# Attention phase of a macaron block: another schedule of units, projections, sums and rotation on four engines

## The chip, the cores and the metric

The kernel runs on one core of one Trainium2 chip. The metric is the device time of one execution in microseconds. The engines are called as the profile calls them: PE (TensorE), DVE (VectorE), ACT (ScalarE), POOL (GpSimd) and SP (the queue that issues all DMAs here).

## The reference

The block computes, on x of 8 x 512 x 512 in fp32:

```python
x = x + 0.5 * ffn(layernorm(x))          # 2:4-sparsified SwiGLU, 512 -> 2048 -> 512
x = x + attention(layernorm(x))
x = x + 0.5 * ffn(layernorm(x))

# attention, 16 heads of 32, one shared key/value head
q = (x @ w_q.T) heads * 32**-0.5;  k, v = split(x @ w_kv.T);  k *= 32**-0.5
q, k = rotary_xpos(q, scale), rotary_xpos(k, 1 / scale)
out = softmax(where(causal, -max, q @ k.T)) @ v
out = out @ w_proj.T + b_proj
```

## The kernel before

Three phases follow one another: `ffn_phase`, `attention_phase`, `ffn_phase`. The change touches the second alone.

**Units.** The attention of one batch element (a "batch", B of 8) is 16 units. Four consecutive units are one group: four heads whose head dimensions fill the 128 partitions (`HG` = 4 heads, `NHG` = 4 groups a batch). Unit K of a group has one block of 128 query rows, row i = K % 4, against (i+1)·128 keys, so the four units of a group have 128, 256, 384 and 512 keys. K runs on through all batches (`ALL` = 128).

**One unit, engine by engine.** `scores(K)` (L871) is four fp32 matmuls, one per head, into banks 0 to 3 of PSUM; they wait until `mask_scores(K-1)` has emptied those banks. `mask_scores(K)` (L1143, DVE, operation at L1149) adds the causal mask, writes the scores to a slot of `probs` and their minimum to `nmax`. `exps(K, s)` (L1023, ACT, L1029) takes the exponential in place and sums the row. `turn_probs(K, j)` (L887, PE, L892) transposes each 128x128 block of the four heads into a turn bank. `copy_turned(K, j)` brings it to `pt`, on ACT (L1034) or, where `ON_VECTOR` says so, on DVE (L1155). `weigh(K)` (L895, matmuls L907) multiplies by the values into bank 6.

**The group's end.** `invert_sums` (DVE, L1161) takes the reciprocal of 16 sums, `widen` (ACT, L1040) spreads them to 128x512, `turn_sums` (PE, L868) transposes them, `drain_sums` (ACT, L1047) copies the result to `rt`, `scale_output` (DVE, L1168) multiplies bank 6 by `rt` into `att`. `cast_output` (ACT, L1051) and `low_output` (POOL, L764) split `att` into a high and a low part. The first `weigh` of the next group waits for `scale_output`.

**Side work.** While a batch is computed, PE also projects the next batch's keys/values (L826) and queries (L851, four row tiles) and the previous batch's output (L918, four row tiles): nine items of 12 matmuls 128x512. All go through one PSUM bank, `spare`. Each unit has four places (`side(K, 0..3)`); an item has a period of six places, with three matmuls in each of the first four. DVE empties `spare`: `rotate_q` (L1110 to L1112, three multiplications out of the bank, then an addition on POOL, L759) or `add_output` (L1173); ACT does it for the keys/values (L1005). The next item waits for that (`take_spare`). LayerNorm of the next batch (normalise, `turn_x`, high part on ACT at L242, low part on DVE at L237) sits in units 0 and 1 of each batch, four `turn_x` in all.

**Turn banks.** Banks 4 and 5 alternate for everything that PE transposes (`next_turn`, `take_turn`). A transpose waits until the bank's previous content has been drained, by whichever engine drains it.

**What sets the order.** Every engine has its own list of instructions, written out by hand in a function `step(K)`, and executes it strictly in that order. PE's step K is: side 0, [`turn_sums` of the previous group if i = 0], `turn_probs` 0 and 1, side 1, `weigh(K-1)`, `turn_probs` 2 and 3, side 2, `scores(K+2)`, side 3, then the turns of x, keys or queries. ACT's step K has the exponentials of K+1 with the copies of K between them; DVE's has the copies of K, then `mask_scores(K+2)`, and `scale_output` last if i = 0.

The lines that set the places:

```python
ON_VECTOR = ((), (1,), (1,), (1,))
TURN_X, TURN_KV, TURN_K, TURN_Q = (0, 1), 3, 6, (10, 11)
ROTATE = {5: 0, 6: 1, 8: 2, 9: 3}
SUM = {11: 0, 12: 1, 14: 2, 15: 3}
STATS = {7: (0,), 10: (1,), 13: (2, 3)}
```

Of the kernel before, what the change touches and what calls it, by code (L numbers as in the profile page):

```python
# [18 lines left out]
F32 = mybir.dt.float32  # L19
# [6 lines left out]
P = 128  # L26
# [4 lines left out]
def macaron_kernel(nc, x_in, w_gu, w_d, w_q, w_kv, w_p, b_p, rotary, out):  # L31
# [40 lines left out]
    nmax = place("nmax", [P, 2, TT], F32)  # L72
# [62 lines left out]
    with ExitStack() as ctx:  # L135
# [51 lines left out]
        q_done = sem("q_done")  # L187
        q_rotated = sem("q_rotated")
# [454 lines left out]
        def attention_phase(src, dst, m0):  # L643
# [27 lines left out]
            def blocks_before(K, of):  # L671

                one = [sum(1 for j in range(i + 1) if of(i, j)) for i in range(TT)]
                return K // TT * sum(one) + sum(one[:K % TT])
# [10 lines left out]
            def copies_of(K, j):  # L685

                mine = by_vector if by_vector(K % TT, j) else by_scalar
                return (pt_vector if mine is by_vector else pt_scalar,
                        blocks_before(K, mine) + sum(1 for n in range(j + 1) if mine(K % TT, n)))
# [10 lines left out]
            for hg in range(NHG):  # L700
                next_turn(("q", 0, hg))
            for K in range(ALL):
                nxt, k = K // UNITS + 1, K % UNITS
                if k % TT == 0 and K > 0:
                    next_turn(("r", K // TT - 1))
                for j in range(K % TT + 1):
                    next_turn(("p", K, j))
                if nxt < BATCHES:
                    if k in TURN_X:
                        next_turn(("x", nxt, 2 * k))  # L710
                        next_turn(("x", nxt, 2 * k + 1))
# [4 lines left out]
                    if k in TURN_Q:  # L716
                        next_turn(("q", nxt, 2 * (k - TURN_Q[0])))
                        next_turn(("q", nxt, 2 * (k - TURN_Q[0]) + 1))
            next_turn(("r", ALL // TT - 1))

            with nc.Block() as blk:
# [30 lines left out]
                def _(g):  # L752
# [4 lines left out]
                    def finish_q(B, t):  # L757
                        g.wait_ge(q_rotated, (B * TT + t + 1) * QSTEP)
                        g.tensor_tensor(qrot[:, t], qrot[:, t], qtmp[:, t % 2], ALU.add).then_inc(q_finished, 1)  # L759

                    def low_output(G):
                        h_of, l_of = att_of(G // NHG)
                        g.wait_ge(att_h_done, G + 1)
                        g.tensor_tensor(l_of[:, G % NHG], att[:, :], h_of[:, G % NHG].bitcast(F32), ALU.subtract).then_inc(att_l_done, 1)  # L764

                    def step(K):
                        B, k = divmod(K, UNITS)
                        nxt = B + 1
                        if k % TT == 1 and K > TT:
                            low_output(K // TT - 1)  # L770
                        if nxt < BATCHES:
                            if k == 3:
                                for t in range(TT):
                                    add_bias(nxt, t)
                            if k in ROTATE:
                                finish_q(nxt, ROTATE[k])
                        if k == 13 and B + 2 < BATCHES:
                            ln_gpsimd(g, B + 2 + m0, 0)
# [16 lines left out]
                def _(pe):  # L795
# [25 lines left out]
                    def project_kv(B, k):  # L821
                        if k == 0:
                            pe.wait_ge(xnt_done, (B + m0) * TT + TT)
                            take_spare(kvt_done, B + 1)
                        for n, (w, x) in enumerate(((wkv_h, xnt_h), (wkv_l, xnt_h), (wkv_h, xnt_l))):
                            last = pe.matmul(spare[0:2 * HD, :], w[:, k], x[:, 0, k], start=(k == n == 0),  # L826
                                             stop=(k == KD - 1 and n == 2))
                        if k == KD - 1:
# [17 lines left out]
                    def project_q(B, t, k):  # L846
                        if k == 0:
                            take_spare(q_rotated, (B * TT + t + 1) * QSTEP)
                        tok = slice(t * P, (t + 1) * P)
                        for n, (x, w) in enumerate(((xnt_h, wq_h), (xnt_h, wq_l), (xnt_l, wq_h))):  # L850
# [462 lines left out]
```

## Time and profile before

| | us |
|---|---|
| median of 3 runs | 2982.3 (2977.7 to 2983.5) |
| the profiled execution | 2983.71 |
| its span | 2981.9 |
| PE busy | 2794.2 (94%) |
| DVE busy | 1855.5 (62%) |
| ACT busy | 1200.8 (40%) |
| POOL busy | 157.0 (5%) |

The span runs from the first to the last instruction. Busy times overlap between engines. PE's clock is at one of two levels, 2.4 GHz (written 1.00) or 1.2 GHz (0.50); a row shows the mean of a stretch. The first FFN phase ends at about 1091 us, the attention ends at about 1891 us.

### The profile page before, as it was taken

Reading aid. Unit: us, or ns where it says so; the run is one execution under the profiler, and the core shown is the slowest. Engines: PE = TensorE matmul, PEld = TensorE weight load, DVE = VectorE, ACT = ScalarE, POOL = GpSimd, SP = SyncE. Lnnn points to the kernel's source line nnn. Section 1 sums busy time; section 2 is a strip of 40 time slices with the busy share of each in tenths; the row PEclk is TensorE's granted clock in tenths of the full one; section 3 lists DMA queues with packets and bytes.
Section 4 is the critical chain, followed back from the end, with each engine's and each line's share of the span. In section 5 each row is a group of like instructions: output and inputs, shape, how many; then the busy total and the mean of one; then the engine's idle time right before and its main releaser. Section 6 shows DMA issues by size and latency. Waiting matters only on the chain. (4 is left out here: it accounts for less than half of the span.)

```text
span 2981.9 us, 41915 instructions
## 1 busy us (share of the span) xinstructions
PE 2794.2 (94%) x15648; PEld 2213.2 (74%) x15648; DVE 1855.5 (62%) x3535; ACT 1200.8 (40%) x2527; POOL 157.0 (5%) x152
## 2 busy tenths in 40 slices
PE   7999999999999977788888887799999999999998
PEld 6888888888888855556555655588888888888887
DVE  5666666666756646555555555476766576676665
ACT  3323233333332315666666677233333333333232
POOL 0000000000000003111111110000000000000000
PEclk9999999999999988999999999899999999999999
DMA  3211211221121020000000000321131112112100
GB/s 131 82 43 57 85 43 46 79 96 49 53 75 43 14 108 1 1 29 11 20 30 29 15 8 16 120 75 49 46 127 43 42 58 85 50 46 90 56 14 29
DMA packets 65021, 156.11 MB, mean 52 GB/s; under 512 B 6864, under 2 KB 6992, under 8 KB 64592
## 3 DMA queue, kind: packets, MB, share of 16 engines
q1 hardware_dynamic: 64848, 153.77, 15.2%
q8 instruction: 112, 1.84, 0.3%
q14 instruction: 61, 0.50, 0.1%
HBM read 128.58 MB, written 25.17 MB: 52 GB/s over the span
## 5 line engine op out<-in xcount | busy, mean ns | idle before, releaser
L346 PE MATMUL bank<-xnt_h,wgu_h 128*128 128x512 f32 x2048 | 803.3, 392 | 10.3 <-issue 7.4
L346 PE MATMUL bank<-xnt_h,wgu_l 128*128 128x512 f32 x2048 | 798.9, 390 | 0.0
L346 PE MATMUL bank<-xnt_l,wgu_h 128*128 128x512 f32 x2048 | 798.4, 390 | 0.0
L503 DVE TENSOR_TENSOR h<-bank,sg 128x512 f32<-128x512 f32 x256 | 176.9, 691 | 600.4 <-PE bank L346 585.9
L346 PEld LDWEIGHTS bank<-xnt_h,wgu_h 128*128 128x128 f32 x2048 | 385.6, 188 | 91.5 <-issue 9.0
L442 ACT ACTIVATE mag<-h 128x512 f32<-128x512 f32 x256 | 162.0, 633 | 702.6 <-DVE h L503 702.6
L346 PEld LDWEIGHTS bank<-xnt_h,wgu_l 128*128 128x128 f32 x2048 | 385.3, 188 | 80.3
L346 PEld LDWEIGHTS bank<-xnt_l,wgu_h 128*128 128x128 f32 x2048 | 385.7, 188 | 79.2
L365 PE MATMUL bank<-wd_h,hs_h 128*128 128x512 f32 x1024 | 400.5, 391 | 9.1 <-DVE hs_l L538 9.1
L365 PE MATMUL bank<-wd_l,hs_h 128*128 128x512 f32 x1024 | 400.1, 391 | 0.0
L365 PE MATMUL bank<-wd_h,hs_l 128*128 128x512 f32 x1024 | 400.0, 391 | 0.0
L1149 DVE CUSTOM_DVE_ANT_0 probs<-bank,causal 128x384 f32<-128x384 f32 (+3 forms) x512 | 220.7, 487 | 230.2 <-PE bank L883 229.2
L450 ACT CAST hs_h<-h 128x512 fp32r<-128x512 f32 x256 | 155.5, 622 | 508.1 <-DVE h L532 508.1
L1029 ACT ACTIVATE probs<-probs,nmax 128x384 f32<-128x384 f32 (+3 forms) x512 | 286.4, 562 | 91.2 <-DVE nmax L1149 91.1
L438 ACT ACTIVATE sg<-bank 128x512 f32<-128x512 f32 x256 | 153.0, 598 | 215.6 <-PE bank L346 214.8
L892 PE MATMUL bank<-ident,probs 128*128 128x128 f32 x1280 | 185.7, 285 | 49.2 <-DVE xnt_l L237 33.1
L365 PEld LDWEIGHTS bank<-wd_h,hs_h 128*128 128x128 f32 x1024 | 193.3, 189 | 50.3 <-DVE hs_l L538 9.9
L365 PEld LDWEIGHTS bank<-wd_l,hs_h 128*128 128x128 f32 x1024 | 193.4, 189 | 40.4
L365 PEld LDWEIGHTS bank<-wd_h,hs_l 128*128 128x128 f32 x1024 | 193.3, 189 | 40.1
L892 PEld LDWEIGHTS bank<-ident,probs 128*128 128x128 f32 x1280 | 148.3, 145 | 90.0 <-ACT probs L1029 38.9
L1034 ACT COPY pt<-bank 128x512 f32<-128x512 f32 x224 | 130.4, 583 | 117.9 <-PE bank L892 117.7
L490 DVE SCALAR_TENSOR_TENSOR x_sb<-bank,x_sb 128x512 f32<-128x512 f32 (+1 forms) x256 | 159.2, 682 | 22.9 <-PE bank L365 22.9
(105 smaller groups left out, 3090.7 us busy)
## 6 DMA issues: line engine op xcount, KB each, us to landing
raw_gu<-in_w_gu SPq DMA_DIRECT2D x128, 512.0 KB, 5.0
raw_d<-in_w_d SPq DMA_DIRECT2D x128, 256.0 KB, 2.6
x_mid<-x_sb SPq DMA_DIRECT2D x64, 256.0 KB, 2.0
x_sb<-in_x SPq DMA_DIRECT2D x32, 256.0 KB, 4.9
x_sb<-x_mid SPq DMA_DIRECT2D x8, 1024.0 KB, 5.8
x_sb<-x_mid SPq DMA_DIRECT2D x32, 256.0 KB, 5.1
out<-x_sb SPq DMA_DIRECT2D x32, 256.0 KB, 2.1
probs<-in_w_q SPq DMA_DIRECT2D x1, 1024.0 KB, 4.8
```

The costliest lines, as they stand in the source:

```text
L346: last = pe.matmul(ps, w[:, r, kind, k], xs[:, b, k], start=(i == 0), stop=(i == 3 * KD - 1))
L365: last = pe.matmul(bank[DOWN + t][:, :], hs[:, b, r, tok], w[:, r], start=(i == 0), stop=(i == 3 * NR - 1))
L438: a.activation(sg[:, r % 2], bank[GATE + r % 2][:, :], ACT.Silu).then_inc(silu_done, 1)
L442: a.activation(mag[:, r], h[:, r], ACT.Abs).then_inc(mag_done, 1)
L450: a.copy(hs_h[:, b, r], h[:, r]).then_inc(hs_h_done, 1)
L490: v.scalar_tensor_tensor(out=x, in0=bank[DOWN + t][:, :], scalar=0.5, in1=x, op0=ALU.mult, op1=ALU.add).then_inc(added, 1)
L503: v.tensor_tensor(h[:, r], bank[UP + r % 2][:, :], sg[:, r % 2], ALU.mult).then_inc(h_done, 1)
L892: last = pe.transpose(ps[:, s * P:(s + 1) * P], probs[:, K % 2, s, j * P:(j + 1) * P], ident[:, :])
L1029: a.activation(row, row, ACT.Exp, bias=nmax[:, K % 2, s:s + 1], scale=-1.0, accum_out=sums[:, G % 2, s, i:i + 1]).then_inc(exp_done, 1)
L1034: a.copy(pt[:, K % 2, j], bank_of["p", K, j][:, :].rearrange("p (s n) -> p s n", n=P)).then_inc(pt_scalar, 1)
L1149: v.tensor_tensor_reduce(out=probs[:, K % 2, s, 0:w], in0=bank[SCORES + s][:, 0:w], in1=causal[:, S - w:S], scale=1.0, scalar=MASKED, op0= ...
```

## The change

- `AHEAD = 3`: `scores(K+3)` is issued in step K (was K+2), `mask_scores(K+3)` and `exps(K+2)` likewise, so `probs` and `nmax` have three slots. `qt` has one slot instead of two. The order of the rows stays 0, 1, 2, 3.
- The fourth block of the longest row (j = 3) is copied by DVE, not by ACT.
- Each projection item is split in five parts of 2, 2, 3, 2 and 3 matmuls (was four of 3), with a period of seven places, from place 0 of unit 0 (was place 2 of unit 2).
- `turn_x` is for the batch after next, one in each of units 11 to 14; the turns of queries are at units 10 and 12.
- The query rotation goes to POOL: DVE copies the bank to `qraw` (one instruction), POOL does the three multiplications and the addition. Batch 0 keeps the old way.
- `widen` and both halves of the output split go from ACT to POOL.
- The sums: `invert_sums` at the end of DVE's third step of a group, `widen` in POOL's third step, `turn_sums` at the start of PE's fourth step, ahead of the transposes of the longest row (before: a step later, after the group).
- In front of batch 0, the four `turn_x` of batch 1 stand between the turns of queries and `scores(0..2)`.

The diff, cut to its core:

```diff
-    nmax = place("nmax", [P, 2, TT], F32)
+    nmax = place("nmax", [P, 3, TT], F32)
...
-    qtmp = place("qtmp", [P, 2, D], F32)
-    qt = place("qt", [P, 2, NHG, S], F32)
+    qraw = place("qraw", [P, 2, D], F32)
+    qtmp = place("qtmp", [P, D], F32)
+    qt = place("qt", [P, NHG, S], F32)
-    probs = place("probs", [P, 2, HG, S], F32)
+    probs = place("probs", [P, 3, HG, S], F32)
...
-            ON_VECTOR = ((), (1,), (1,), (1,))
-            TURN_X, TURN_KV, TURN_K, TURN_Q = (0, 1), 3, 6, (10, 11)
-            ROTATE = {5: 0, 6: 1, 8: 2, 9: 3}
-            SUM = {11: 0, 12: 1, 14: 2, 15: 3}
-            STATS = {7: (0,), 10: (1,), 13: (2, 3)}
+            AHEAD = 3
+            ORDER = (0, 1, 2, 3)
+            ON_VECTOR = ((), (1,), (1,), (1, 3))
+            TURN_X, TURN_KV, TURN_K, TURN_Q = {11: 0, 12: 1, 13: 2, 14: 3}, 1, 4, {10: (0, 1), 12: (2, 3)}
+            PERIOD, PARTS = 7, 5
+            STATS = {3: 0, 5: 1, 7: 2, 8: 3}
+            ROTATE = {3: 0, 5: 1, 6: 2, 8: 3}
+            SPARE_FREE = {}
+            for n in range(1, 1 + 2 * TT):
+                k, place_in = divmod(n * PERIOD + PARTS - 1, 4)
+                SPARE_FREE[(k, place_in) if place_in < 3 else (k + 1, 0)] = n
...
+                    def rotate_q(B, t):
+                        n = B * TT + t
+                        g.wait_ge(q_copied, n - TT + 1)
+                        g.wait_ge(q_finished, n)
+                        if t == 0:
+                            g.wait_ge(qt_turned, B * NHG)
...
+                        g.tensor_tensor(heads_of(qrot[:, t]), q, cos, ALU.mult).then_inc(q_rotated, 1)
+                        g.tensor_tensor(tmp[:, :, 0:HALF], q[:, :, HALF:HD], sin[:, :, 0:HALF], ALU.mult).then_inc(q_rotated, 1)
+                        g.tensor_tensor(tmp[:, :, HALF:HD], q[:, :, 0:HALF], sin[:, :, HALF:HD], ALU.mult).then_inc(q_rotated, 1)
+                        finish_q(B, t)
+
+                    def widen(G):
+                        g.wait_ge(rsum_done, G + 1)
+                        if G > 0:
+                            g.wait_ge(r_turned, G)
+                        g.tensor_copy(rwide[:, :, :, :], rsum[:, :, :].rearrange("p h t -> p t h").unsqueeze(3)
+                                      .to_broadcast([P, TT, HG, HD])).then_inc(rwide_done, 1)
+
+                    def part_output(G):
                         h_of, l_of = att_of(G // NHG)
+                        g.wait_ge(att_done, G + 1)
+                        g.tensor_copy(h_of[:, G % NHG], att[:, :]).then_inc(att_h_done, 1)
                         g.wait_ge(att_h_done, G + 1)
                         g.tensor_tensor(l_of[:, G % NHG], att[:, :], h_of[:, G % NHG].bitcast(F32), ALU.subtract).then_inc(att_l_done, 1)
...
                         if k % TT == 1 and K > TT:
-                            low_output(K // TT - 1)
+                            part_output(K // TT - 1)
+                        if k % TT == 2:
+                            widen(K // TT)
                         if nxt < BATCHES:
-                            if k == 3:
+                            if k in ROTATE:
+                                rotate_q(nxt, ROTATE[k])
+                            if k == 11:
                                 for t in range(TT):
                                     add_bias(nxt, t)
...
+                    def part_of(part):
+
+                        every = [(k, n) for k in range(KD) for n in range(3)]
+                        return every[part * len(every) // PARTS:(part + 1) * len(every) // PARTS]
...
-                        at = (k - 2) * 4 + place - 2
-                        what, part = divmod(at, 6)
-                        if at < 0 or part >= KD or what > 2 * TT:
+                        what, part = divmod(k * 4 + place, PERIOD)
+                        if part >= PARTS or what > 2 * TT:
                             return
...
                         side(K, 0)
-                        if i == 0 and K > 0:
-                            turn_sums(K // TT - 1)
+                        if k % TT == TT - 1:
+                            turn_sums(K // TT)
                         turn_probs(K, 0)
...
                         side(K, 2)
-                        if K + 2 < ALL:
-                            scores(K + 2)
-                        side(K, 3)
+                        if nxt + 1 < BATCHES and k in TURN_X:
+                            turn_x(nxt + 1, TURN_X[k])
...
+                        if K + AHEAD < ALL:
+                            scores(K + AHEAD)
+                        side(K, 3)
+                        if nxt < BATCHES:
+                            for hg in TURN_Q.get(k, ()):
+                                turn_q(nxt, hg)
...
+                    for t in range(TT):
+                        turn_q(0, t)
+                        turn_x(1, t)
+                        if t < AHEAD:
+                            scores(t)
...
+                        exps(K + AHEAD - 1, 0)
+                        if k % TT == TT - 1:
+                            drain_sums(K // TT)
                         for s in range(1, HG):
                             if s - 1 < len(mine):
                                 copy_turned(K, mine[s - 1])
-                            if s == 2 and i == 1 and K > TT:
-                                cast_output(K // TT - 1)
-                            exps(K + 1, s)
+                            exps(K + AHEAD - 1, s)
...
+                    def copy_q(B, t):
+                        n = B * TT + t
+                        v.wait_ge(q_done, n + 1)
+                        v.wait_ge(q_finished, TT if B == 1 and t < 2 else n - 1)
+                        v.tensor_copy(qraw[:, t % 2], spare[:, :]).then_inc(q_copied, 1)
...
+                        free_spare(K, 0)
+                        if nxt + 1 < BATCHES and k - 1 in TURN_X:
+                            lo_x(nxt + 1, TURN_X[k - 1])
+                        if 1 in ON_VECTOR[i]:
+                            copy_turned(K, 1)
+                        free_spare(K, 1)
...
+                        if 3 in ON_VECTOR[i]:
+                            copy_turned(K, 3)
...
+                        free_spare(K, 2)
+                        mask_scores(K + AHEAD)
+                        if k % TT == TT - 2:
                             invert_sums(K // TT)
...
+                        if k % TT == 0 and K > 0:
                             scale_output(K // TT - 1)
```

`free_spare(K, stage)` calls `copy_q` or `add_output` at the places in `SPARE_FREE`.

## Rows read from the trace of the kernel before

**Rows 1.** The page, its first line.

```profile
span 2981.9 us, 41915 instructions
...
```

**Rows 2.** Windows: us, busy (instructions) of PE, PEld, DVE, ACT, POOL; PEclk, DMA.

```profile
...
1091.10:1226.60 135.50, 98.71 (x804) 65.58 (x804) 77.51 (x235) 73.72 (x197) 30.83 (x27) 0.85 0.13 47
1226.60:1326.30 99.70, 85.71 (x776) 57.38 (x772) 54.69 (x185) 63.35 (x180) 16.34 (x14) 0.91 0.03 12
...
1519.40:1615.10 95.70, 81.22 (x776) 55.48 (x772) 54.65 (x185) 63.36 (x181) 16.37 (x14) 0.96 0.06 23
...
1710.70:1801.30 90.60, 78.42 (x776) 53.52 (x772) 51.91 (x177) 63.31 (x180) 15.11 (x12) 1.00 0.04 13
1801.30:1891.10 89.80, 70.60 (x744) 49.47 (x740) 44.41 (x150) 58.62 (x166) 5.08 (x4) 1.00 0.09 33
...
```

**Rows 3.** Waits of PE over batches 2 to 5: engine, line, releaser: us, times, longest.

```profile
...
PE bank L892 <- DVE xnt_l L237: 20.2, 12, 2.4
PE bank L918 <- DVE x_sb L1173: 10.5, 4, 2.6
PE bank L851 <- DVE qtmp L1112: 8.0, 8, 1.3
PE bank L907 <- DVE att L1168: 5.6, 8, 1.0
PE bank L868 <- ACT rwide L1040: 5.4, 4, 1.4
...
PE bank L892 <- ACT probs L1029: 1.5, 4, 0.4
...
```

**Rows 4.** Timeline at 1502 us: start, us, engine, line, operation [idle before].

```profile
...
1502.08 0.69 DVE L1168 TENSOR_TENSOR att<-bank,rt 128x512 f32<-128x512 f32 x1
...
1502.91 0.43 PE L907 MATMUL bank<-pt,kvtok 128*32 128x128 f32 x8 [0.36 <-DVE att L1168]
...
1504.16 1.14 PE L883 MATMUL bank<-kt,qt 32*128 32x512 f32 x8
...
1505.23 0.50 PE L918 MATMUL bank<-wp_h,xnt_h 128*128 128x512 f32 x1
...
1505.37 0.69 DVE L1149 CUSTOM_DVE_ANT_0 probs<-bank,causal 128x512 f32<-128x512 f32 x1 [2.01 <-PE bank L883]
1505.57 0.39 PE L918 MATMUL bank<-wp_l,xnt_h 128*128 128x512 f32 x1
...
1507.82 1.28 DVE L218 BATCH_NORM_STATS2 stats<-x_sb 128x6 f32<-128x512 f32 x2
...
```

**Rows 5.** Timeline at 1519 us: the sums of a group.

```profile
...
1519.55 0.42 DVE L1149 CUSTOM_DVE_ANT_0 probs<-bank,causal 128x256 f32<-128x256 f32 x1 [1.81 <-PE bank L883]
...
1520.17 0.61 ACT L1040 COPY rwide<-rsum 128x512 f32<-128x512 f32 x1
...
1520.84 0.66 PE L868 MATMUL bank<-ident,rwide 128*128 128x128 f32 x4 [1.36 <-ACT rwide L1040]
...
1520.93 1.00 DVE L231 TENSOR_SCALAR xn<-x_sb,meanvar,rstd 128x512 f32<-128x512 f32 x2
...
1521.53 0.59 ACT L1047 COPY rt<-bank 128x512 f32<-128x512 f32 x1 [0.25 <-PE bank L868]
...
```

**Rows 6.** Groups by line over the attention: busy us, mean ns, idle before.

```profile
...
L1161 DVE RECIPROCAL rsum<-sums 128x16 f32<-128x16 f32 x32 | 8.0, 249 | 6.9 <-ACT probs L1029 6.9
...
L1112 DVE TENSOR_TENSOR krot<-kvtok,rot 128x64 f32<-128x64 f32 x8 | 1.8, 219 | 0.0
...
L780 POOL MEMSET causal<- 128x512 f32 x1 | 0.5, 524 | 309.0 <-POOLq L272 309.0
...
```

**Rows 7.** Timeline at 1118 us: DVE beside POOL.

```profile
...
1118.42 1.29 POOL L759 TENSOR_TENSOR qrot<-qrot,qtmp 128x512 f32<-128x512 f32 x1 [20.08 <-DVE qtmp L1112]
1118.45 1.34 DVE L1111 TENSOR_TENSOR krot<-kvtok,rot 128x64 f32<-128x64 f32 x1
...
```

**Rows 8.** Timeline at 1136 us: the low part of the projection weights.

```profile
...
1136.48 3.23 DVE L1107 TENSOR_TENSOR wp_l<-raw_p,wp_h 128x2048 fp32r<-128x2048 f32 x1
...
```

More of the change, by code:

```diff
@@ L671, in blocks_before @@
             def blocks_before(K, of):
-                one = [sum(1 for j in range(i + 1) if of(i, j)) for i in range(TT)]
+                one = [sum(1 for j in range(i + 1) if of(i, j)) for i in ORDER]
                 return K // TT * sum(one) + sum(one[:K % TT])
@@ L685, in copies_of @@
             def copies_of(K, j):
-                mine = by_vector if by_vector(K % TT, j) else by_scalar
+                i = row_of(K)
+                mine = by_vector if by_vector(i, j) else by_scalar
                 return (pt_vector if mine is by_vector else pt_scalar,
-                        blocks_before(K, mine) + sum(1 for n in range(j + 1) if mine(K % TT, n)))
+                        blocks_before(K, mine) + sum(1 for n in range(j + 1) if mine(i, n)))
             bank_of = {}
@@ L882, in scores @@
                             rows = slice(s * HD, (s + 1) * HD)
-                            last = pe.matmul(bank[SCORES + s][:, 0:width(i)], qt[rows, B % 2, hg, i * P:(i + 1) * P],
+                            last = pe.matmul(bank[SCORES + s][:, 0:width(i)], qt[rows, hg, i * P:(i + 1) * P],
                                              kt[rows, B % 2, 0:width(i)], start=True, stop=True)
@@ L997, in _ @@
                     for t in range(TT):
-                        for k in range(KD):
-                            project_out(BATCHES - 1, t, k, bank[SCORES + t])
+                        for part in range(PARTS):
+                            project_out(BATCHES - 1, t, part, bank[SCORES + t])
                 @blk.scalar
@@ L1054, in step @@
                         B, k = divmod(K, UNITS)
-                        i, nxt = k % TT, B + 1
-                        mine = [j for j in range(i + 1) if by_scalar(i, j)]
+                        nxt = B + 1
+                        mine = [j for j in range(row_of(K) + 1) if by_scalar(row_of(K), j)]
                         if nxt < BATCHES:
+                            if k == TURN_KV:
+                                drain_kv(nxt)
                             if k == TURN_KV + 1:
@@ L1173, in add_output, with free_spare @@
                         v.tensor_tensor(x_of(B, t), x_of(B, t), ps[:, :], ALU.add).then_inc(x_summed, 1)
+                    def free_spare(K, stage):
+                        B, k = divmod(K, UNITS)
+                        n = SPARE_FREE.get((k, stage))
+                        if n is None:
+                            return
+                        if n <= TT:
+                            if B + 1 < BATCHES:
+                                copy_q(B + 1, n - 1)
+                        elif B > 0:
+                            add_output(B - 1, n - 1 - TT, spare)
@@ L1185, in step @@
-                        for j in ON_VECTOR[i]:
-                            copy_turned(K, j)
-                        if nxt < BATCHES:
-                            if k in ROTATE:
-                                rotate_q(nxt, ROTATE[k])
-                            if k == TURN_KV + 1:
-                                keys(nxt)
-                        if B > 0 and k in SUM:
-                            add_output(B - 1, SUM[k], spare)
-                        mask_scores(K + 2)
-                        if B + 2 < BATCHES:
-                            for t in STATS.get(k, ()):
-                                stat(B + 2, t)
-                            if k == 13:
-                                ln_aggregate(v, B + 2 + m0, 0)
-                            if k == UNITS - 1:
-                                normalise(B + 2, 0)
-                                normalise(B + 2, 1)
```

216 lines of the change are left out of this document (106 added, 110 removed).

## The prediction, made before the change was run

> **What bounds the kernel now.** I read the windows first, then PE's waits, then the timeline. The windows [rows 2] cut the attention at the end of each batch's last `scores` slot. The reader is to see that PE is the fullest engine of every batch: in the settled batch 1519.4 to 1615.1 it is busy for 81.2 of 95.7 us, ACT for 63.4, DVE for 54.7, POOL for 16.4. So no engine is full, and PE loses 95.7 - 81.2 = 14.5 us a batch to waits. The wait view over batches 2 to 5 [rows 3] says which (a quarter of each sum is one batch): the turn bank that x holds until DVE has taken its low part, 5.1; `spare`, 2.6 behind `add_output` and 2.0 behind the rotation; the first `weigh` of a group behind `scale_output`, 1.4; `turn_sums` behind `widen`, 1.4. Behind the exponentials PE stands only 0.4 us a batch. That is the row that matters: three units ahead lengthens the lead of the exponentials, and there is next to nothing to win by that alone in a settled batch. The change is decided by its new waits.
>
> The profiled execution took 2983.7 us, 1.8 more than its span [rows 1] and 1.4 more than the median of 2982.3. I sum against 2983.7. A difference within 0.2% (6 us) counts as none.
>
> **What goes.** The waits on x in units 0 to 3 (5.1 a batch) and on `spare` (2.6 + 2.0) go: x is turned one tile at a time, and an item of side work is now followed by two free places, in which PE has other work while DVE empties `spare` with one instruction of 0.69. The copy replaces three multiplications on DVE; DVE and ACT get lighter, which costs and gains nothing by itself, since neither bounds a batch [rows 2].
>
> **Side work in fifths.** 45 blocks of matmuls in place of 36. A block's first matmul holds PE 0.11 longer than the next (0.50 against 0.39 [rows 4]). 9 x 0.11 = **+1.0** a batch.
>
> **Waits added.** I time them from S, the end of PE's `scores` slot. In [rows 4] `scores` start at 1504.16, PE's next work at 1505.23 (= S), the first mask at 1505.37 = S + 0.14; four masks of 512 keys take 1507.82 - 1505.37 = 2.45. Four of 256 keys take 1520.93 - 1519.55 = 1.38 [rows 5]. PE's own work between two points goes by slots read in the same way (start to next start): two transposed blocks 0.9, one 0.44, a side block of two 0.62, of three 0.85.
>
> *Sums.* `turn_sums` of a group now stands in front of the longest row's transposes, one step earlier. From S of the group's third step: 0.14 + 1.38 masks + 0.25 reciprocal [rows 6] + 0.07 + `widen` + 0.06 to PE (ACT's `rwide` ended 1520.78, PE began 1520.84 [rows 5]) = 1.9 + w. The trace has no copy on POOL. Its bounds: a memset of the same 128x512, 0.52 [rows 6], and an addition with two inputs, 1.29 [rows 7]. A copy reads one input, so I take the middle, w = 0.9: ready at S + 2.8. PE arrives with only side 3 and side 0 done: at 0.85, 0.62, 2.3 and 1.4 (in units 3, 7, 11, 15, by which of the places are busy). Waits 1.95 + 2.2 + 0.5 + 1.4 = **6.05** a batch (1.4 before).
>
> The Trainium skill's page GPSIMD Engine Reference, section 3.1, gives 769 ns for a one-input loop over 512 elements; by that, called an estimate, each wait would be 0.13 shorter, 4 us over the kernel. No run here shows it.
>
> *rt.* The second transpose of the longest row needs the bank of the sums: 0.69 after `turn_sums` begins ACT copies `rt`, 0.59 long [rows 5]; ready at 1.34 + a little, PE there at 0.89. 4 x 0.45 = **1.8**.
>
> *att.* The first `weigh` of a group needs `scale_output`, which now stands behind the masks of the longest row (before: of 384 keys). 0.14 + 2.45 + 0.83 (1502.08 to 1502.91 [rows 4]) = S + 3.4. PE arrives at 2.3, 1.5, 2.9 in units 1, 5, 9: **3.5** (1.4 before).
>
> *x and q.* In unit 12 the second turn of queries needs the bank of x, which DVE frees only in its next step, behind masks and `scale_output`: 0.14 + 2.45 + 0.69 + 0.69 = 3.97; PE is there at 0.85 + 0.41. **2.7**, and 0.9 more in unit 14, where ACT is late.
>
> Sum 6.05 + 1.8 + 3.5 + 3.6 = 15.0. PE's busy time in the window contains the tail of the last matmul before each wait, some 0.2 each for 11 waits. Settled batch: 81.2 - 2.2 + 1.0 + 15.0 = **95.0**, 0.7 less than 95.7. For batches 1 to 5: **-3.5**.
>
> **The ends.** Start: the four turns of x, their low parts and the cut of the projection weights, 3.23 on DVE [rows 8], now lie between the first three masks, and one more unit is scored before step 0; with one low part of 0.69 the path is 3.9 longer: +4. Batch 0 has no output projection, so PE arrives earlier at the same latency chains; its waits are 21.5, and from step 0 on it takes about 85 against 82: +3. Together **+7**. Batch 6 has no x left to turn: -1.8 work, -3.6 waits, so 86.8 against 90.6 [rows 2]: **-3.8**. Batch 7 has few sides, but sums no longer at its very end: waits 18, work 66.8 + 0.5, so 85.5 to 86 against 89.8 [rows 2]: **-3.8**.
>
> Off PE's path: POOL gets per batch four rotations (1.29 + two halves + 1.29 [rows 7], halves between 0.65 and 1.29 each: 3.9 to 5.2), four copies and four `widen`, 16.4 + 21 = about 37 of 95 us. Its list stays ahead of what needs it; tightest is unit 6, where the rotation of unit 5 ends at about the S from which `widen` is due 1.8 later. DMA: the load of batch B+4 is now needed in unit 3 instead of 7, and is issued once the last sum is stored, near the end of unit 15, three units ahead of its need: hidden.
>
> Sum: -3.5 + 7 - 3.8 - 3.8 = -4. **2983.7 - 4 = 2980 us**, no measurable change. Own range of this case 2965 to 2998 (w between its bounds moves it by 0.38 x 32 = 12 either way, the rest is how exactly PE's arrival is known).
>
> **Rivals.**
>
> *POOL becomes the late one (0.18).* Place: `turn_sums`. If w is 1.29, each of 32 waits is 0.39 longer: +12. If the halves of a rotation cost 1.29 each, the chain in unit 6 slips by about 1.2 in each of 7 batches: +8. 3000 us. For: POOL's two-input operations are nearly twice as long as DVE's 0.69. Against: about 60% of its time stays free. It decides from w > 1.1.
>
> *POOL blocks DVE (0.08).* At 1118.42 POOL's addition of 1.29 ran; DVE's 64-element multiplication with both inputs in SBUF began at 1118.45 and took 1.34, where its twin of the same size takes 0.22 [rows 6, 7]. DVE has five such or wide instructions in `keys` and four normalisations a batch, each can wait 1.1; if half of them stand before masks that PE waits for, 4 x 1.1 x 7 = +31: 3011 us. Against: in the walk POOL is idle at `keys`, and only the normalisations of units 11 and 13 meet it, with slack behind them. The Trainium skill's page SBUF — State Buffer, section Who interferes with whom, has it as a rule: the port pair shared by DVE and GpSimd is an exclusive lock, for DVE instructions with two SBUF inputs among others; by this rule, the trace agrees, one of the two stands for the other's whole instruction.
>
> *PE's clock falls more often (0.06).* In batch 1 the clock is 0.91 and PE busy 85.7; in the settled batch 0.96 and 81.2; in batch 6 1.00 and 78.4 [rows 2]. Longer single waits (2.8 against 2.6 before) could bring every batch to 0.91: 4.5 x 6 = +27, 3007 us.
>
> *The lead works (0.20).* If `widen` costs 0.52 and the more even side work keeps the clock at 1.00: -12 and -2.8 x 5 = -14 on top: 2954 us. Full success, in which PE waits about 4 us a batch, would be 2983.7 - 7 x 10 = 2914; for it speaks nothing but the removed waits, against it the four chains above.
>
> *The change does nothing (in the forecast).* The third slot itself addresses 0.4 us a batch; the forecast is this plus exchanged waits.
>
> **Chances.** Forecast 0.48, of which 0.18 faster than 2976, 0.20 within, 0.10 slower than 2988; the lead works 0.20, all faster; POOL late 0.18, blocked 0.08, clock 0.06, all slower. Faster 0.38, same 0.20, slower 0.42. Range 2954 to 3010: it takes in the rivals' prices and leaves out full success and a block or clock loss beyond theirs, together about 2 in 10.
>
> **What would show it.** Right: PE's waits name `rwide` (about 6 us a batch, up to 2.2 each), `att` (3.5), the copy of `rt` (1.8); the waits on `x_sb` and `qtmp` are gone; `xnt_l` remains near 3 before the turns of queries; PE busy near 82. POOL's copy near 0.9, POOL busy near 37 a batch. Wrong: `turn_sums` not waiting, waits on exponentials or on `pt` copies that I put at nothing, a clock off 0.96, or DVE instructions lengthened beside POOL.

## The result, and the profile after

The changed kernel takes 2996.65 us (median of 5 runs, 2991.64 to 2998.23) against 2979.88 for the kernel before on the same chip: a ratio of 1.0049, interval 1.0038 to 1.0061. It is slower by 17 us, 0.5%. The prediction said 2980, no measurable change. 2996.65 lies inside its range of 2954 to 3010, but it forecast 4 us less and took up to 6 us either way as no change; measured are 17 us more.

The profiled execution took 2995.57 us, 11.9 more than the one before. The first line of its page and the lines of busy time, to be read beside [rows 1]:

```profile
span 2993.8 us, 41971 instructions
...
PE 2809.6 (94%) x15648; PEld 2218.4 (74%) x15648; DVE 1864.9 (62%) x3511; ACT 1152.8 (39%) x2432; POOL 268.5 (9%) x299
```

Windows of the kernel after, cut as in [rows 2] at the end of each batch's last `scores` slot: the first holds the prologue and batch 0, then come batches 1, 2, 4, 6 and 7.

```profile
1091.10:1244.50 153.40, 106.82 (x832) 71.19 (x832) 84.78 (x247) 73.83 (x202) 43.78 (x46) 0.84 0.11 41
1244.50:1341.00 96.50, 84.19 (x777) 56.45 (x773) 55.70 (x181) 56.91 (x167) 31.99 (x34) 0.95 0.05 15
1341.00:1436.10 95.10, 82.66 (x776) 55.30 (x772) 55.68 (x181) 57.15 (x168) 31.99 (x34) 0.96 0.07 23
1531.20:1627.70 96.50, 84.20 (x776) 56.47 (x772) 55.67 (x181) 57.31 (x168) 32.01 (x34) 0.95 0.06 22
1722.90:1810.80 87.90, 78.58 (x760) 52.48 (x756) 47.83 (x165) 54.96 (x164) 30.56 (x32) 0.98 0.04 13
1810.80:1904.70 93.90, 75.53 (x732) 52.76 (x728) 45.80 (x146) 49.20 (x143) 10.01 (x12) 0.93 0.09 32
```

The reader is to see three things. The settled batches take 95.1 to 96.5 us, as before (95.7). The last batch takes 93.9 where it took 89.8, at a clock of 0.93 where it was 1.00. And the first window is longer: 153.4, against 135.5 before. PE's waits in batches 2 to 5 of the kernel after, the answer to [rows 3] (us in total, times, longest):

```profile
PE bank L920 <- POOL rwide L794: 18.2, 16, 1.8
PE bank L959 <- DVE att L1214: 15.2, 12, 1.9
PE bank L913 <- DVE xnt_l L239: 10.1, 4, 2.5
PE bank L944 <- ACT rt L1091: 2.6, 11, 0.2
PE bank L944 <- DVE xnt_l L239: 2.6, 4, 0.7
```

The waits on `x_sb` and on the rotation are gone. In their place PE waits for `rwide` at the end of every group and for `att` at the start of every group but a batch's last: 33.4 of the 48.7 us. Where the wait for `rwide` comes from is seen in unit 2 of a group (timeline of the kernel after, the answer to [rows 5]):

```profile
1379.70 0.42 DVE L1195 CUSTOM_DVE_ANT_0 probs<-bank,causal 128x256 f32<-128x256 f32 x1 [1.15 <-PE bank L935]
...
1381.08 0.25 DVE L1207 RECIPROCAL rsum<-sums 128x16 f32<-128x16 f32 x1
1381.39 0.61 POOL L794 COPY rwide<-rsum 128x512 f32<-128x512 f32 x1 [3.76 <-DVE rsum L1207]
...
1382.06 0.66 PE L920 MATMUL bank<-ident,rwide 128*128 128x128 f32 x4 [1.76 <-POOL rwide L794]
```

The sums had been complete before (in e1 below the reciprocal stands in front of the masks, and DVE still has no idle time ahead of it). The reciprocal of 0.25 us stands behind four masks that nothing in this group needs, and PE stands 1.76 us.

### The profile page after: what moved, and what is told of

Same layout as the page of the kernel before. It is cut to its first block and busy times, and to the rows that moved or that the text cites. A ratio compares the mean times of both kernels' runs of the same rounds, so it can differ in the third digit from the quotient of the medians.

```text
span 2993.8 us, 41971 instructions
## 1 busy us (share of the span) xinstructions
PE 2809.6 (94%) x15648; PEld 2218.4 (74%) x15648; DVE 1864.9 (62%) x3511; ACT 1152.8 (39%) x2432; POOL 268.5 (9%) x299
## 5 line engine op out<-in xcount | busy, mean ns | idle before, releaser
L348 PEld LDWEIGHTS bank<-xnt_l,wgu_h 128*128 128x128 f32 x2048 | 385.6, 188 | 78.8
L944 PE MATMUL bank<-ident,probs 128*128 128x128 f32 x1280 | 200.6, 295 | 12.5 <-ACT rt L1091 5.6
L944 PEld LDWEIGHTS bank<-ident,probs 128*128 128x128 f32 x1280 | 155.4, 150 | 63.0 <-issue 23.9
L1201 DVE COPY pt<-bank 128x512 f32<-128x512 f32 x128 | 88.2, 689 | 168.1 <-PE bank L944 168.1
```

Of the source, the lines that this page charges most:

```text
L348: last = pe.matmul(ps, w[:, r, kind, k], xs[:, b, k], start=(i == 0), stop=(i == 3 * KD - 1))
L944: last = pe.transpose(ps[:, s * P:(s + 1) * P], probs[:, K % 3, s, j * P:(j + 1) * P], ident[:, :])
L1201: v.tensor_copy(pt[:, K % 2, j], bank_of["p", K, j][:, :].rearrange("p (s n) -> p s n", n=P)).then_inc(pt_vector, 1)
```

## Experiments

Every kernel was timed four to eight times beside the kernel before on the same chip; the median of the kernel before was 2979.9 to 2982.4 there.

**What do the two new waits cost?** One line of DVE's list is moved in each kernel.

```diff
 # e1_sums, DVE's step(K), from the kernel after
+                        if k % TT == TT - 2:
+                            invert_sums(K // TT)
                         free_spare(K, 1)
...
                         mask_scores(K + AHEAD)
-                        if k % TT == TT - 2:
-                            invert_sums(K // TT)
```

> The changed kernel with the reciprocal of a group's sums taken one mask earlier on DVE (in the group's third step before the masks of K+3, not after). Its wait on rwide at turn_sums sums to about 39 us over the kernel (18.2 in four settled batches, 7.1 in batch 0, 5.9 in batch 7, the rest in the others). Theory A, the changed kernel loses by latency chains at the group's end that PE stands in: that wait goes almost wholly and 25 to 35 us of the time with it, so that the kernel is at 2962 to 2972 us, faster than the kernel before. Rival B, PE runs into the next wait (bank of rt, att, x) whatever is removed: under 8 us of gain. Both: the copy on GpSimd stays at 0.61 us.

```diff
 # e2_att, DVE's step(K), from the kernel after
+                        if k % TT == 0 and K > 0:
+                            scale_output(K // TT - 1)
                         free_spare(K, 2)
                         mask_scores(K + AHEAD)
...
-                        if k % TT == 0 and K > 0:
-                            scale_output(K // TT - 1)
```

> The changed kernel with scale_output ahead of the masks of the longest row in DVE's first step of a group, not behind them. PE's wait on att sums to about 31 us (15.2 in four settled batches, 4.2 in batch 0, 5.8 in batch 7). Theory A: that wait goes and 20 to 28 us with it, 2969 to 2977 us; the wait on x before the second turn of queries in unit 12 shrinks by up to 0.7 a batch as well. Rival B: under 8 us.

Measured: e1 2942.28 us, ratio to before 0.9878 (0.9862 to 0.9894); e2 2955.47, 0.9921 (0.9910 to 0.9933). So the first is worth 54 us and the second 41, in the changed kernel; both are above what was expected (25 to 35 and 20 to 28). PE's waits in the whole attention, of the kernel after:

```profile
PE bank L920 <- POOL rwide L794: 40.3, 31, 2.4
PE bank L959 <- DVE att L1214: 32.9, 24, 2.4
PE bank L913 <- DVE xnt_l L239: 15.9, 6, 3.3
```

and of e1:

```profile
PE bank L959 <- DVE att L1214: 32.8, 24, 2.4
PE bank L913 <- DVE xnt_l L239: 15.9, 6, 3.3
PE bank L944 <- DVE xnt_l L239: 10.5, 12, 1.7
```

One wait is gone. Of its 40.3 us, 6.0 came back at L944 behind `xnt_l` (4.5 to 10.5) and 1.5 there behind `rt` (5.6 to 7.1). Yet the kernel is 54 us faster. The rest is in PE's own rows. The window of the whole attention from the end of step 0, first of the kernel after, then of e1:

```profile
1156.10:1904.70 748.60, 640.22 (x6021) 431.59 (x6017) 422.39 (x1384) 444.63 (x1300) 230.60 (x246) 0.95 0.06 19
```

```profile
1155.80:1850.10 694.30, 619.13 (x6021) 421.56 (x6017) 420.19 (x1384) 444.75 (x1299) 231.32 (x246) 0.97 0.06 21
```

The same 6021 matmuls are busy for 640.2 and for 619.1 us: of the 54.3 us that the window shortens, 21.1 are busy time. Part of it is the tail that the records count before a wait (31 waits of 0.2 by the prediction's estimate, 6 us). The rest fits the clock. The stretches that the trace has at 0.50 add up to 71.7 us in this window of the kernel after and to 41.0 in that of e1. Work that takes all of such a stretch would take half of it at 1.00, so 30.7 us less of them are worth at most 15.4, an estimate; 6 and 15 make the 21. Here the removed wait gave back its own length, and PE's other work ran at the lower clock for a shorter time. That the clock follows a removed wait upward is no rule, as e11 below shows.

**Do the two add up?** Both lines moved, `scale_output` as in e2 and the reciprocal as in e1.

> The changed kernel with both moves on DVE: the reciprocal ahead of the masks in a group's third step (e1) and scale_output ahead of the masks in its first step (e2). Apart they gave 54 and 41 us, more than the waits they removed (40 and 33), while the time at half clock fell from 75 to 44 us in each. Theory A (each wait is a stall of its own, and part of the gain is the clock): 2901 us if they add up in full; 2905 to 2920 us if the clock's part comes only once; a settled batch near 84.5 us. Rival B: behind both stands one common wait (the bank of x before the turns of queries, or the bank of rt), so that together they give little more than e1: over 2932 us.

Measured: 2913.01 us, 0.9775 (0.9761 to 0.9788), 84 below the changed kernel; 95 would be the plain sum. PE's waits in the attention of e5:

```profile
PE bank L913 <- DVE xnt_l L239: 12.3, 6, 2.7
PE bank L944 <- DVE xnt_l L239: 11.6, 12, 1.7
PE bank L935 <- DVE nmax L1195: 7.7, 13, 1.7
PE bank L944 <- ACT rt L1091: 7.2, 26, 0.7
PE bank L882 <- ACT pt L1085: 5.0, 7, 0.7
```

With nothing large in front, small waits come up: for the masks (`nmax`) 7.7, for ACT's copies 5.0.

**Undoing one part of the change.** e10 is the kernel after with the sums alone in their old place, one step later for all four engines; `widen` stays on POOL.

```diff
-                if k % TT == TT - 1:
-                    next_turn(("r", K // TT))
+                if k % TT == 0 and K > 0:
+                    next_turn(("r", K // TT - 1))
...
-                        if k % TT == 2:
+                        if k % TT == 3:
                             widen(K // TT)
...
-                        if k % TT == TT - 1:
-                            turn_sums(K // TT)
+                        if k % TT == 0 and K > 0:
+                            turn_sums(K // TT - 1)
...
+                        if k % TT == TT - 1:
+                            invert_sums(K // TT)
                         free_spare(K, 0)
```

> The changed kernel with one part undone: the sums of a group in their old place (reciprocal at the start of the fourth step, widening after it, turn_sums at the start of the next group); everything else as changed, scale_output behind the masks too. Theory: of all that the change does, the early place of the sums is what costs the time, since it asks for the reciprocal behind the masks; then this is as fast as e1, 2938 to 2948 us, some 50 us below the changed kernel and well below the kernel before. Rival: in the old place the copy of rt comes later, scale_output with it, and the wait on att grows by what is won: 2965 us or more.

Measured: 2948.51 us, 0.9885 (0.9870 to 0.9899), 48 below the changed kernel and 34 below the one before. One part of the change, as it is placed, thus turns the whole from a gain into a loss. Its waits in the attention:

```profile
PE bank L960 <- DVE att L1217: 32.9, 24, 2.4
PE bank L945 <- DVE xnt_l L239: 24.2, 18, 2.2
PE bank L914 <- DVE xnt_l L239: 15.8, 6, 3.3
```

It lies half a microsecond above the 2938 to 2948 that were expected. The wait for `rwide` is gone, but the one at the transposes behind `xnt_l` grows from 4.5 to 24.2; in e1 it grew to 10.5 only, and e1 is 6 us faster.

**Is the early place of the sums worth anything?** e6 is e5 with the sums as in e10.

> e5 with the sums of a group back in their old place (reciprocal and widening in the fourth step, turn_sums at the start of the next group, where the row has a single transposed block), the lead left at three. If the early place of the sums is worth something by itself: slower than e5 by 3 us or more. If it only costs the wait for the copy of rt in front of the second transpose of the longest row (0.2 per group in the trace, 6 us over the kernel): the same or up to 6 us faster.

Measured: 2913.72 us, 0.9779 (0.9765 to 0.9792), as e5 within 1 us. With both waits mended the early place buys nothing; what it did in the changed kernel was to cost, by the masks put ahead of the reciprocal. (With the wait for `att` left in, e1 is 6 us ahead of e10.)

**Is the lead of three units worth anything?** e7 is e6 with one number changed, the slots left at three.

```diff
-            AHEAD = 3
+            AHEAD = 2
```

> e6 with the lead back at two units (scores, masks and exponentials as in the kernel before), so that e6 against e7 is the third unit alone. As the prediction had it, the kernel before waited 0.4 us a batch for the exponentials, so the lead is worth nothing: within 5 us of e6. Rival: that held at 95.7 us a batch only; at about 85 a batch the exponentials of the next unit are no longer done when PE asks for them, and e7 is 15 to 40 us slower than e6, with PE waiting on the exponentials.

Measured: 2928.21 us, 0.9824 (0.9810 to 0.9837): 14.5 slower than with three, above the 5 us that were expected and just short of the rival's 15. PE's waits in the attention, of e7:

```profile
PE bank L945 <- DVE xnt_l L239: 28.5, 18, 2.7
PE bank L945 <- ACT probs L1082: 16.5, 24, 1.7
PE bank L914 <- DVE xnt_l L239: 9.1, 6, 2.1
```

and of e6:

```profile
PE bank L945 <- DVE xnt_l L239: 25.4, 18, 2.2
PE bank L914 <- DVE xnt_l L239: 12.3, 6, 2.7
PE bank L936 <- DVE nmax L1198: 5.8, 10, 1.4
```

The wait for the exponentials is 16.5 us over the attention of e7, and with a lead of three it is not among the waits. In the kernel before it was 0.4 us in a settled batch and 8.1 over the attention, 4.7 of it in batch 7. The prediction looked at the settled batches alone and read the 0.4 as "next to nothing to win"; part of it was hidden behind the other waits.

**Does it matter where the rotation runs?** e9 is e5 with the three multiplications back on DVE, out of the bank; the addition stays on POOL.

```diff
-                        v.tensor_copy(qraw[:, t % 2], spare[:, :]).then_inc(q_copied, 1)
+                        cos = rot[:, t, 0].unsqueeze(1).to_broadcast([P, HEADS, HD])
+                        sin = rot[:, t, 1].unsqueeze(1).to_broadcast([P, HEADS, HD])
+                        rotate(heads_of(spare[:, :]), heads_of(qrot[:, t]), heads_of(qraw[:, t % 2]), cos, sin, q_rotated)
```

> e5 with the rotation of queries back on DVE in all batches (three multiplications out of the bank, the addition on GpSimd), at the same places. DVE gets 28 times 0.75 us more, GpSimd 28 times 2.8 less. If DVE's list is not what PE waits for: within 4 us of e5. If each rotation delays the masks or copies behind it and those PE: 5 to 20 us slower.

Measured: 2914.49 us, 0.9776 (0.9763 to 0.9789). The difference to e5 is 1.5 us, less than can be measured (e5 2912.1 to 2917.0, e9 2910.6 to 2915.1): with the two lines moved, this part of the change is neutral.

**The start.** The trace of the kernel after shows DVE's normalisations lengthened beside POOL's additions, and the first exponential late (timeline of the prologue):

```profile
1133.84 5.30 POOL L765 TENSOR_TENSOR x_sb<-x_sb,bias 128x512 f32<-128x512 f32 x4
1133.95 2.84 DVE L233 TENSOR_SCALAR xn<-x_sb,meanvar,rstd 128x512 f32<-128x512 f32 x2 [1.64 <-issue]
...
1137.98 1.45 DVE L233 TENSOR_SCALAR xn<-x_sb,meanvar,rstd 128x512 f32<-128x512 f32 x1
...
1150.28 0.40 ACT L1080 ACTIVATE probs<-probs,nmax 128x128 f32<-128x128 f32 x1
...
1151.98 1.12 PE L944 MATMUL bank<-ident,probs 128*128 128x128 f32 x4 [1.53 <-ACT probs L1080]
```

The row `ACT L1029` of the kernel before that answers to the fourth of these began at 1140.19. Two causes offer themselves: the lengthened normalisations (e3 takes the additions away), and the order of ACT's list, in which four `hi_x`, each behind a low part on DVE, stand ahead of the exponentials (e4 puts the whole x chain behind them).

```diff
 # e3_bias, POOL's list, from the kernel after
+                        if K == 9:
+                            for t in range(TT):
+                                add_bias(0, t)
...
-                    for t in range(TT):
-                        add_bias(0, t)
                     for K in range(ALL):
                         step(K)
```

> The changed kernel with the four additions of the bias for batch 0 on GpSimd moved from in front of unit 0 to unit 9. In front of unit 0 three normalisations take 2.84 + 1.45 us beside them, where alone they take about 0.54 each. If DVE is held by GpSimd there and stands on the path: the start of unit 0 comes 2 to 2.7 us earlier and the time falls by as much. If the long normalisations are hidden: no change, within 1.5 us.

```diff
 # e4_start, ACT's list, from the kernel after; PE's and DVE's alike
                     for t in range(TT):
                         drain_q(0, t)
-                        hi_x(1, t)
                     for K in range(AHEAD - 1):
                         for s in range(HG):
                             exps(K, s)
+                    for t in range(TT):
+                        hi_x(1, t)
```

> The changed kernel with the start in another order: the turns of queries, the first three scores, their masks and the first exponentials come first, the four turns of x of batch 1 with their high and low parts after them; the cut of the projection weights comes last, and PE waits for it in batch 1. Theory: the changed kernel ends its step 0 at 1156.1 us where the kernel before ends it at 1144.5, since ACT takes the first exponential behind four high parts of x that each wait for DVE. Then 5 to 9 us come back. Rival: the chain of the four x tiles is as long wherever it stands, since the projection of keys in unit 0 needs them: under 3 us.

Measured: e3 3002.36 us, 1.0083 (1.0070 to 1.0097): slower than the changed kernel by 6, the expectation missed. e4 2992.62, 1.0050 (1.0036 to 1.0064): 4 faster, between the 5 to 9 of its theory and the 3 of its rival.

In e3 the normalisations have their short length back (timeline of DVE):

```profile
1133.52 1.00 DVE L233 TENSOR_SCALAR xn<-x_sb,meanvar,rstd 128x512 f32<-128x512 f32 x2 [1.65 <-issue]
...
1136.66 0.54 DVE L233 TENSOR_SCALAR xn<-x_sb,meanvar,rstd 128x512 f32<-128x512 f32 x1
```

Two take 1.00 instead of 2.84, one 0.54 instead of 1.45. The masks behind them are 2.2 us earlier, but step 0 ends only 1.0 earlier (1155.1 against 1156.1). The additions came back elsewhere; PE's waits of e3 in batch 0 begin with

```profile
PE bank L921 <- POOL rwide L794: 10.6, 4, 4.8
```

where the kernel after has 7.1 with 2.4 as the longest: four additions of 1.32 in unit 9 stand ahead of `widen` in unit 10. Here POOL does become the late one, as that rival has it, but in a place that the experiment made.

In e4 the exponentials begin at 1140.02, as early as before the change, and step 0 still ends at 1154.1. PE's timeline says why:

```profile
1148.97 0.69 PE L874 MATMUL bank<-xnt_h,wkv_h 128*64 128x512 f32 x1 [1.40 <-DVE xnt_l L239]
```

The first side item, now in unit 0, needs all four tiles of x. In the kernel after it begins at 1149.79, right behind the last low part of x, and in e4 at 1148.97: in both orders the chain of x holds it. A later first item was not tried.

**The kernel before with the same repair.** `scale_output` moved ahead of the masks, as in e2, nothing else.

> The kernel before with scale_output ahead of the masks in DVE's first step of a group. Its PE waits on att for about 16 us in all (8.4 in batches 1 to 6, 2.4 in batch 0, 4.6 in batch 7). If a removed wait comes back whole there too: 10 to 16 us less, 2965 to 2971 us, and less half-clock time. If the copy of rt, which in this kernel is asked for in the same step, now holds DVE in front of the masks: no gain, or slower by up to 5 us.

Measured: 2973.11 us, 0.9972 (0.9962 to 0.9983): 7 to 9 us faster than the kernel before, just short of the 10 that were the least expected. Its waits in the attention:

```profile
PE bank L892 <- DVE xnt_l L237: 26.7, 18, 2.3
PE bank L851 <- DVE qtmp L1112: 17.0, 13, 1.9
PE bank L918 <- DVE x_sb L1173: 14.8, 7, 2.6
PE bank L892 <- ACT probs L1029: 13.7, 19, 1.7
```

The wait for `att`, 15.5 us in the kernel before, is gone, but the rotation's grew from 13.4 to 17.0 and the one for the exponentials from 8.1 to 13.7. The clock went the other way than in e1. From the end of step 0 to the end of the attention, first the kernel before, then e11:

```profile
1144.50:1891.10 746.60, 629.30 (x6052) 429.07 (x6048) 419.29 (x1422) 497.27 (x1408) 115.28 (x98) 0.96 0.06 19
```

```profile
1143.30:1884.70 741.40, 636.54 (x6052) 435.96 (x6048) 422.71 (x1422) 495.55 (x1408) 115.48 (x98) 0.95 0.06 19
```

PE's idle time fell from 117.3 to 104.9, but the same 6052 matmuls are busy for 7.2 us longer, and the stretches at 0.50 add up to 77.3 us in place of 57.4, worth up to 10 us. Less time at half clock was expected and did not come. So a removed wait can give back more than its length (e1, e2) or less (e11), and no run here shows what decides.

Moving `scale_output` alone thus explains 7 to 9 of the 69 us by which e5 lies below the kernel before; the rest comes from the rest of the change. The kernel before also waits 13.5 us for `rwide`; the like move for that wait was not tried there.

**The best version.** e12 is e5 with the start of e4 and the turns of queries split 3 and 1, so that the second turn in unit 12, whose bank DVE frees late, goes.

```diff
-            ... {10: (0, 1), 12: (2, 3)}
+            ... {10: (0, 1, 2), 12: (3,)}
```

> e5 with the start of e4 and the third turn of queries moved from unit 12 to unit 10, so that in unit 12 a single turn of queries follows and takes the other bank. e4 gave 4 us; the wait on x before the turns of queries in unit 12 is 12.3 us over six batches in e5. If both are waits of their own: 2898 to 2906 us, the wait named gone. If the wait only moves to the first transpose of unit 13, which then needs that bank: 2907 to 2911 us.

Measured: 2903.3 us, 0.9737 (0.9725 to 0.9750), faster than both kernels, by 77 to 79 us and by 93. A settled batch of it:

```profile
1317.10:1401.00 83.90, 78.79 (x777) 53.21 (x780) 55.06 (x182) 57.10 (x168) 32.14 (x34) 1.00 0.08 27
```

PE is busy for 78.8 of 83.9 us at full clock. Over the attention the wait at L913 (12.3 in e5) is gone, but the one at the transposes behind `xnt_l` grew from 11.6 to 20.6 and is the largest left. e12 makes two edits at once on e5; how its 9.7 us divide between them was not measured.

## Why the prediction was wrong

The walk through the settled batch held. What failed are the terms for the two ends: "+4" for the start, where the trace has 11.6 more, and "-3.8" for batch 7, where it has 4.1 more. Together they miss by 15.5 of the 17.6 us between -4 and +13.6. The prediction's terms, beside what the traces of before and after show (a batch from the end of its predecessor's last `scores` slot to its own):

| | predicted | measured |
|---|---|---|
| start, to the end of step 0 | +4 | 1144.5 to 1156.1: +11.6 |
| batch 0 | +3 | 82.1 to 88.4: +6.3 |
| batches 1 to 5 | -3.5 | -5.7 |
| batch 6 | -3.8 | 90.6 to 87.9: -2.7 |
| batch 7 | -3.8 | 89.8 to 93.9: +4.1 |
| sum | -4 | +13.6 (the whole execution +11.9) |

**Right.** The walk through the settled batch gave 95.0; batches 2, 3 and 5 took 95.1 to 95.2, batches 1 and 4 96.5. PE was busy for 82.7 in batch 2 where it said near 82, and the waits on `x_sb` and `qtmp` went. Its waits include a tail of 0.2 each that the wait view counts as busy; taken alike, a batch has `rwide` 5.25 against 4.6, the copy of `rt` 1.0 against 0.65, `att` 2.9 against 3.8, the turn of queries 2.5 against 2.5. So `widen` (0.61 on POOL, not 0.9) and `rt` were too high and `att` too low by about as much; that the sum came out so near is in part luck. The -5.7 comes almost wholly from batches 1 and 2 (99.7 to 96.5, 97.4 to 95.1), to which the prediction gave the 0.7 of a settled batch; batches 3 to 5 moved by -0.6, +0.8 and -0.4.

**Wrong, the start: "+4".** Its 3.9 is the cut of the projection weights, 3.23, and one low part, 0.69, both on DVE. The cut was no addition: in the kernel before it already stands between the masks of unit 0 and those of unit 1, which begin at 1139.63 ([rows 8]), and after the change it takes 2.28. What does lengthen the path was left out. On ACT the first exponentials stand behind four `hi_x` and begin at 1150.28, not 1140.19, and PE's first transposes stand behind them. The first side item needs all of x and now lies in step 0; five of its matmuls stand between those transposes and `scores`, for 2.3 us. e4 takes ACT's order away and brings the end of step 0 forward by 2.0, e3 the long normalisations, by 1.0. The rest no run took away; in e4 PE stands for x three times ahead of the side item, for 2.4, 0.4 and 1.4.

**Wrong, batch 7: "-3.8".** It took waits of 18 and work of 67.3, in terms that count the tails as waits. Before, they were 19.2 + 19 x 0.2 = 23.0, so it took 5 us of waits away. Measured are 93.9 - 75.5 = 18.4 of idle time in some 15 waits, 21.4 with the tails, and 72.5 of work. Of the waits, `rwide` has 5.9 (before 5.3) and `att` 5.8 (before 4.6). The larger miss is the work, 5.2 us. Before, PE's clock was 1.00 all through this batch; after, 13.7 us of it are at 0.50, which is worth at most 6.8. The first such stretch begins behind two waits of 2.4 (`att` at 1817.64, then `rwide`):

```profile
1820.03 0.66 PE L944 MATMUL bank<-ident,probs 128*128 128x128 f32 x4
...
1823.76 1.05 PE L920 MATMUL bank<-ident,rwide 128*128 128x128 f32 x4 [2.43 <-POOL rwide L794]
```

Four transposes take 0.66 before it and 1.05 in it; the clock is 1.00 from 1810.8 to 1823.7 and 0.50 from 1823.9 to 1827.3. Before the change, PE's waits in this batch for the sums, for `att` and for the exponentials were at most 1.6. The prediction carried the busy time of before over, as if the clock were a property of the work. It did so in batch 6 too: its 86.8 takes a clock of 1.00 for granted, and it was 0.98. In batch 0 its waits of 21.5 held (18.9 of idle time and the tails), the work was 3 us more than its 63.5, with 13.7 us at 0.50 against 9.6 before.

**The rivals.** *POOL late*: no. `widen` at 0.61 is far from 1.1. *POOL blocks DVE*: only in the prologue, about 1 us. *The clock falls more often*: this happened, but in the first and last batch and not in the middle ones, where the prediction put it and priced it. *The lead works*: what it needed, `widen` at 0.52 and a clock of 1.00, was not there; the changed kernel with a lead of two was not run. Its full-success figure, 2914, is near what e5 measures (2913.0), but e5 is another kernel, and its start is 10.7 us later than before, which the figure does not count. For it spoke, in the prediction's words, "nothing but the removed waits"; those were what counted. The prediction found both new waits by place and cause, priced them nearly right, and went on to the sum; it did not ask whether they belonged to the idea or to the order of two lines.

Open: why the clock rises with the removed waits of e1 and e2 and falls in e11. Which part among the fifths, the x turns one by one and ACT's lighter load carries most of the gain of e7 over the kernel before (53 us, of which `scale_output` alone gives 7 to 9 there) was not tried part by part.

## What to carry to other kernels

When an engine with a handwritten order gets longer work in front of a short instruction that the fullest engine waits for (here a reciprocal of 0.25 us and a multiplication of 0.69 behind four masks), move the short one ahead first, and judge the idea after that: two moved lines made 84 us here, in a change that had lost 17. A wait that is near nothing in the trace (the exponentials' 0.4 in a settled batch) may be covered by the others; a longer lead against it was worth 14.5 us here once they were gone. Price a first and a last batch by their own lists, not as a difference to the settled one. And where a wait goes into the fullest engine's list or out of it, take the clock as a term with a range of its own, from a stretch of the same work at either level: here it added 15 us to one gain and took 10 from another, by the estimates above.

## What was not expected of the hardware

- Removing 40.3 us of PE's waits (31 of them, none above 2.4) took 54 us off the kernel, and removing 32.9 took 41. The granted clock over the attention rose from 0.95 to 0.97 each time, to 0.98 with both, and to 0.99 in e12; PE's busy time for the same 6021 matmuls went from 640.2 to 619.1 (e1) and 608.2 (e12). But in the kernel before, removing 15.5 took off only 7 to 9: the clock went from 0.96 to 0.95.
- POOL's copy of 128x512 with one input took 0.61, a copy on ACT 0.58 to 0.61, one on DVE out of a PSUM bank 0.69, while POOL's multiplications and additions of that size with two inputs took 1.27 to 1.32. So moving `widen` from ACT (0.61 there too) cost nothing in length. The groups of POOL in the attention of the kernel after:

```profile
L772 POOL TENSOR_TENSOR qrot<-qrot,qtmp 128x512 f32<-128x512 f32 x28 | 35.8, 1278 | 2.2
...
L786 POOL TENSOR_TENSOR qtmp<-qraw,rot 128x256 f32<-128x256 f32 x28 | 20.6, 735 | 0.0
...
L794 POOL COPY rwide<-rsum 128x512 f32<-128x512 f32 x32 | 19.5, 609 | 204.0 <-DVE rsum L1207 204.0
```

- A normalisation on DVE (all of it in SBUF) took 0.50 to 0.54 alone and up to 1.45 beside POOL's additions, while the low part of x, which reads a PSUM bank, took its usual 0.69 at 1137.37, beside the same additions (they run from 1133.84 for 5.30). The Trainium skill's page SBUF — State Buffer, section Who interferes with whom, states that DVE and GpSimd share one pair of ports and that it is an exclusive lock; the trace agrees in that e3, without the additions there, gives 1.00 for two normalisations where the kernel after has 2.84.
